# End of the second network: three down projections after the last gate/ups, and the lower parts of three tiles over TensorE

## Chip, cores and metric

One core of a Trainium2 chip. The metric is the device time of one execution in microseconds (us); the median of the runs before is 905.04 us.

## What is computed

x is 4096 rows (2 batches of 2048) of 256 numbers. Three stages follow each other, each on a layernorm of x and each added back to x: a feed-forward network, an attention, and the same feed-forward network again. Only the last stage's end is touched. The network is

```python
def fp4_linear(x, w):
    xq = fp4_quant_dequant(x)      # blocks of 16: scale max|x|/6, round to an 8 value grid
    wq = fp4_quant_dequant(w)
    return jnp.einsum('bsk,nk->bsn', xq, wq)
gate = fp4_linear(x, w_gate)       # 256 -> 704
y = fp4_linear(x, w_up)            # 256 -> 704
h = jax.nn.silu(gate) * y
return fp4_linear(h, w_down)       # 704 -> 256
```

and x becomes x + 0.5 * network(layernorm(x)).

## The kernel before

The rows lie in 32 tiles of 128 (NT = 32). A network (f = 0 or 1) is a software pipeline of rounds c, written by hand for each engine in its own queue; engines meet only at semaphores. In every round "chain" k is the quantised row of tile k's h (704 columns, for its down projection) and, where `ahead(k)` holds (k up to 27), of the normalised x of tile k + 4 (256 columns, for the gate/up of that tile, which is why the gate/up of tile c + 3 reads chain c - 1). Matrix products are made in two parts of reduced precision: an upper part `T_hi` and a lower part `T_lo` of the transposed data, against an upper and a lower part of the weights.

Round c of network 2, by engine:

- TensorE (PE): waits for the lower part of chain c - 1, and for `gu_read` (VectorE has read the gate/up result of tile c + 2, whose PSUM bank is written next); `gate_up` part 0 of tile c + 3 (6 matmuls of 512 columns, L1881); `transpose_chain(c)` (8 transposes, 6 where no x is ahead, L1762); part 1 (6 x 512); where `by_product` holds, `chain_lower(c)` (2 matmuls of 512 columns, L1920, that subtract `T_hi` in PSUM); part 2 (6 x 384); then the down projection of tile c into the single PSUM area `dn` (10 matmuls L1892 on `T_hi`, 7 matmuls L1899). It waits for `down_done`, that is for ScalarE's copy of the previous tile out of `dn`.
- ScalarE (ACT), in this order: `absolute(c+1)` (|y| of chain c + 1, L1407; of tile 31 L1398), `down_out(c-1)` (dn to SBUF, L1414), `chain_upper(c)` (L1425), `silu_gate(c+3)` (L1449), and where `by_product` holds `chain_rest(c)` (L1439, L1441: the lower part out of PSUM).
- VectorE (DVE): `scales(c+2)` (L811 to L824), `to_grid(c+1)` (L833 `rounded`, L839 `grid`), `scaled(c+2)` (L852), `lower(c)` where `by_vector` holds (L894, L896), `product(c+3)` (L798: silu times up, which sets `gu_read`).
- GpSimd (POOL): `residual(c-1)` (x plus down, L554), `quantised(c+1)` (`zq` = grid times scale, L587).
- SyncE: sends finished tiles of x to memory, the last four one by one.

`by_vector` holds in network 2 for chains 0 to 28; chain 29 goes over TensorE and ScalarE. Tiles 30 and 31 are "late": VectorE makes their zq (`quantised_late`, L918, L920) and lower parts (L904 to L910), TensorE's `last_two` does transposes of 30, upper down projection of 30 (L2012), transposes of 31, rest of 30 (L2021), and then both parts of 31 into a bank of its own. VectorE adds tile 31 to x (L927). `T_hi` and `T_lo` have two slots, used by the parity of k. `down_out(t)` also waits until the residual of tile t - 2 is done, because `down` has two slots.

Of the kernel before, what the change touches and what calls it, by code (L numbers as in the profile page):

```python
# [7 lines left out]
F32 = mybir.dt.float32  # L8
# [5 lines left out]
P = 128  # L14
# [16 lines left out]
def macaron_kernel(nc, x_in, wq, bq, wk, bk, wv, bv, wo, bo, w_gate, w_up, w_down, out):  # L31
# [35 lines left out]
    with ctx:  # L67
# [84 lines left out]
        plain.close()  # L152
        sb("slots_ahead_of_xk", [P, RING - 4, QT * P], at=plain)
# [148 lines left out]

        def by_vector(f, k):

            return isinstance(k, int) and (0 if f else 4) <= k < NT - 3
# [148 lines left out]
        def _(pool):  # L454
# [95 lines left out]
            def ffn_step(f):  # L550
# [162 lines left out]
        def _(dve):  # L713
# [77 lines left out]
            def ffn_step(f):  # L791
# [34 lines left out]
                def to_grid(k):  # L826

                    lo, hi = part(k)
                    y_k = z if last(k) else y
                    abs_k = silu[:] if last(k) else yabs_of(f, k, lo, hi)  # L830
# [8 lines left out]
                    nc.vector.scalar_tensor_tensor(out=grid[:, lo:hi], in0=abs_k, scalar=ROUND,  # L839
                                                   in1=rounded[:, lo:hi], op0=ALU.max,  # L840
                                                   op1=ALU.subtract).then_inc(grid_done, 1)
# [47 lines left out]
                def lower(k, par):  # L889
# [4 lines left out]
                    nc.vector.tensor_tensor(out=T_lo[:, par, n, :], in0=bank[:, n, :],  # L894
                                            in1=T_hi[:, par, n, :].bitcast(F32), op=ALU.subtract)
                    nc.vector.tensor_tensor(out=T_hi[HR:P, par, HK + KD, :], in0=bank[HR:P, HK + KD, :],  # L896
                                            in1=T_hi[HR:P, par, HK + KD, :].bitcast(F32),
                                            op=ALU.subtract).then_inc(vector_lo, 1)

                def lower_late(k, par):  # L900
# [3 lines left out]
                    nc.vector.tensor_tensor(out=T_lo[:, par, 0:4, :], in0=bank[:, 0:4, :],  # L904
                                            in1=T_hi[:, par, 0:4, :].bitcast(F32),
                                            op=ALU.subtract).then_inc(late_lo, 1)
                    dve.wait_ge(hi_done, number(f, k))
                    nc.vector.tensor_tensor(out=T_lo[:, par, 4:HK, :], in0=bank[:, 4:HK, :],
                                            in1=T_hi[:, par, 4:HK, :].bitcast(F32), op=ALU.subtract)
                    nc.vector.tensor_tensor(out=T_hi[HR:P, par, HK + KD, :], in0=bank[HR:P, HK + KD, :],  # L910
                                            in1=T_hi[HR:P, par, HK + KD, :].bitcast(F32),
                                            op=ALU.subtract).then_inc(late_lo, 1)

                def quantised_late(k, par):
# [3 lines left out]
                    nc.vector.tensor_tensor(out=blocks(zq[:, 0:I]), in0=blocks(grid[:, 0:I]),  # L918
                                            in1=spread(s_neg[:, par, 0:HB], HB), op=ALU.mult)
                    nc.vector.tensor_tensor(out=blocks(zq[:, I:I + HR]), in0=blocks(grid[:, I - HR:I]),  # L920
# [298 lines left out]
        def _(act):  # L1219
# [172 lines left out]
            def ffn_step(f):  # L1392
# [27 lines left out]
                def chain_upper(k, par):  # L1420
# [4 lines left out]
                    nc.scalar.activation(T_hi[:, par, t, :], bank[:, t, :], ACT.Copy).then_inc(hi_done, 1)  # L1425

                def late_upper(k, par):

                    bank = bank_of(k)
                    act.wait_ge(T_done, number(f, k))  # L1430
                    nc.scalar.activation(T_hi[:, par, 0:4, :], bank[:, 0:4, :], ACT.Copy).then_inc(late_hi, 1)
                    nc.scalar.activation(T_hi[:, par, 4:8:3, :], bank[:, 4:8:3, :], ACT.Copy).then_inc(hi_done, 1)

                def chain_rest(k, par):
# [4 lines left out]
                    last = nc.scalar.activation(T_lo[:, par, t, :], bank[:, t, :], ACT.Copy)  # L1439
                    if hidden(k):  # L1440
                        last = nc.scalar.activation(T_hi[HR:P, par, HK + KD, :], bank[HR:P, HK + KD, :], ACT.Copy)  # L1441
# [20 lines left out]
                def step(c, par):  # L1462
# [7 lines left out]
                    if c == NT - 2:  # L1470
                        down_out(c - 1, 1 - par)
                    if late(c) and chain(c):
                        late_upper(c, par)
                    if extra and c == NT - 1:
                        keys_upper(0, 0)
                    if hidden(c - 1) and c < NT and c != NT - 2:
                        down_out(c - 1, 1 - par)
                    if measured:
# [20 lines left out]
                    if extra and c == -2:  # L1499
                        query_row()  # L1500
                    if by_product(f, c):
                        chain_rest(c, par)
                    if extra and c == NT - 3:
# [252 lines left out]
        def _(pe):  # L1756
# [118 lines left out]
            def gate_up(par, part):  # L1875
# [3 lines left out]
                         for T, w in ((T_hi, w1_hi), (T_hi, w1_lo), (T_lo, w1_hi))]  # L1879
                for n, (T, kd, w) in enumerate(terms):  # L1880
                    last = nc.tensor.matmul(gu[:, lo:hi], lhsT=T[:, par, HK + kd, :], rhs=w[:, kd, lo:hi],  # L1881
# [6 lines left out]
            def project_down_first(par, dn):  # L1888

                terms = [(k, half) for k in range(HK) for half in (0, D)]  # L1890
                for n, (k, half) in enumerate(terms):
                    nc.tensor.matmul(dn, lhsT=T_hi[:, par, k, :], rhs=wd_hl[:, k, half:half + D],  # L1892
                                     start=n == 0, stop=False)

            def project_down_rest(par, dn):

                terms = [(T_hi, HK + KD, HK, half) for half in (0, D)] + [(T_lo, k, k, 0) for k in range(HK)]
                for n, (T, k, wk, half) in enumerate(terms):
                    last = nc.tensor.matmul(dn, lhsT=T[:, par, k, :], rhs=wd_hl[:, wk, half:half + D],  # L1899
# [15 lines left out]
            def chain_lower(f, c, par):  # L1915

                pe.wait_ge(hi_done, number(f, c))
                if hidden(c):
                    for bank in range(2):
                        last = nc.tensor.matmul(bank2[:, bank, :], lhsT=neg_ident[:],  # L1920
                                                rhs=T_hi[:, par, 4 * bank:4 * bank + 4, :],
                                                start=False, stop=True, skip_group_check=True)
                else:
                    last = nc.tensor.matmul(bank2[:, 1, P:3 * P], lhsT=neg_ident[:],
                                            rhs=T_hi[:, par, HK:HK + KD, :],
# [10 lines left out]
            def ffn_step(f):  # L1936
                def step(c, par):
# [7 lines left out]
                    if gated:  # L1945
                        pe.wait_ge(gu_read, NT * f + c + 3)
                        gate_up(1 - par, 0)
                    if gated and c < 0:
                        gate_up(1 - par, 1)
                        gate_up(1 - par, 2)  # L1950
# [15 lines left out]
                    if gated and c >= 0:  # L1966
                        gate_up(1 - par, 1)
# [9 lines left out]
                    if gated and c >= 0:  # L1977
                        gate_up(1 - par, 2)
                    if hidden(c):
                        if f and c == 0:  # L1980
                            pe.wait_ge(x_att, NT)
                        if f or c:
                            pe.wait_ge(down_done, (NT - 1) * f + c)
                        else:
                            pe.wait_ge(wc["lo"], len(groups))
                        pe.wait_ge(hi_done, number(f, c))
                        project_down_first(par, dn)
                        wait_lowered(f, c)
                        project_down_rest(par, dn)
# [13 lines left out]
                def down_late(par, dn):  # L2003
# [4 lines left out]
                    for k in range(HK):  # L2008
                        if k == 4:
                            pe.wait_ge(hi_done, number(f, NT - 2 + par))  # L2010
                        for half in (0, D):
                            nc.tensor.matmul(dn, lhsT=T_hi[:, par, k, :], rhs=wd_hl[:, k, half:half + D],  # L2012
                                             start=k == 0 and half == 0, stop=False)

                def down_late_rest(par, dn):

                    terms = [(T_lo, k, k, 0) for k in range(HK)] + [(T_hi, HK + KD, HK, half) for half in (0, D)]
                    for n, (T, k, wk, half) in enumerate(terms):
                        if n in (0, 4):
                            pe.wait_ge(late_lo, 4 * f + 2 * par + 1 + n // 4)  # L2020
                        last = nc.tensor.matmul(dn, lhsT=T[:, par, k, :], rhs=wd_hl[:, wk, half:half + D],  # L2021
# [50 lines left out]
            gate_up(0, 0)  # L2072
            key_query_lower()
            gate_up(0, 1)
            transpose_chain(0, -3)
            pe.wait_ge(aw["m_lo"], 1)
            gate_up(0, 2)
# [199 lines left out]
            gate_up(0, 0)  # L2277
            gate_up(0, 1)
# [7 lines left out]
            gate_up(0, 2)  # L2286
# [6 lines left out]
            for columns in range(3):  # L2293
                gate_up(1, columns)
# [6 lines left out]
            for columns in range(3):  # L2301
                gate_up(0, columns)
# [26 lines left out]
```

## Time and profile before

| | us |
|---|---|
| median of 3 runs (lowest, highest) | 905.04 (904.86, 905.08) |
| the profiled execution | 904.92 |
| its span, first to last instruction | 903.1 |
| PE / DVE / ACT / POOL busy in the span | 882.2 / 691.0 / 620.8 / 551.2 |

The span is what the trace covers; the execution's own time is 1.8 us more. Busy time is the union of an engine's instructions. Matmuls overlap in the records, so that the distance from one start to the next is their cost, not the duration shown. All times below are from the span's start.

### The profile page before, as it was taken

To read this page: it belongs to the slowest core of one execution; us is meant where nothing else is said; L and a number is where in the kernel's file an instruction comes from. 1 tells how busy PE (TensorE), PEld (TensorE's weight loads), DVE (VectorE), ACT (ScalarE), POOL (GpSimd) and SP (SyncE) were. 2 spreads that over 40 slices of the span, in tenths; PEclk is the share of its full clock that TensorE was granted. 3 is DMA by queue.
4 is the path that set the end of the run, shared out by engine and by line. 5 is a ranking of instruction groups with operands and counts; after the bars stand their busy time and mean duration, and the time that the engine had idled before them with its cause. 6 is when DMAs were issued, how large, how long until landed. Compare 5 with 4: busy or idle time off the path is not lost.

```text
span 903.1 us, 16183 instructions
## 1 busy us (share of the span) xinstructions
PE 882.2 (98%) x5608; PEld 795.6 (88%) x5608; DVE 691.0 (77%) x1086; ACT 620.8 (69%) x1383; POOL 551.2 (61%) x619
## 2 busy tenths in 40 slices
PE   4999999999999999999999999999999999999997
PEld 2789999999988899989998899998998999999996
DVE  7977999999977666555564644545599999999998
ACT  6789888887674765768675576767784667555453
POOL 5477889898420354536752154546577878877762
PEclk9999999999999999999999999999999999999999
DMA  9200000000000000000000000000000000000001
GB/s 314 68 1 1 1 1 2 1 1 1 1 1 0 1 1 1 1 1 2 1 1 1 1 1 1 1 1 1 1 1 1 1 24 24 25 24 24 1 24 47
DMA packets 11952, 13.81 MB, mean 15 GB/s; under 512 B 864, under 2 KB 11104, under 8 KB 11872
## 3 DMA queue, kind: packets, MB, share of 16 engines
q1 hardware_dynamic: 11872, 12.79, 4.3%
q8 instruction: 45, 0.74, 0.3%
q14 instruction: 35, 0.29, 0.1%
HBM read 8.59 MB, written 4.19 MB: 14 GB/s over the span
## 4 chain that ended last, share of the span: by engine, by line
PE 89%; DVE 4%; POOL 3%; issue 2%; ACT 1%; DMA 1%; SPq 0%; DVEq 0%; POOLq 0%
PE bank L1881 25%; PE bank L2137 19%; PE bank_b L1892 7%; PE bank L1762 7%; PE bank_b L1899 5%; PE bank L2175 5%; PE bank L2179 5%; PE bank L2177 5%; PE bank L2100 3%; POOL p_lo L637 2%; PE bank_b L2179 2%; PE bank_b L2175 2%; PE bank_b L2177 2%; PE bank L2118 1%; PE bank_b L2118 1%
## 5 line engine op out<-in xcount | busy, mean ns | idle before, releaser
L637 POOL TENSOR_TENSOR p_lo<-s_ring,p_hi 128x512 fp32r<-128x512 f32 x128 | 167.7, 1315 | 215.8 <-ACT p_hi L1620 215.7
L1004 DVE TENSOR_TENSOR top<-bank,top 128x512 f32<-128x512 f32 x98 | 67.7, 691 | 117.6 <-ACT s_ring L1604 117.6
L587 POOL TENSOR_TENSOR zq<-grid,s_neg 128x256 f32<-128x256 f32 (+2 forms) x184 | 142.0, 799 | 12.6 <-DVE grid L839 12.6
L1881 PE MATMUL bank<-w_hi,T_hi 128*128 128x512 f32 (+1 forms) x384 | 148.6, 387 | 0.4 <-DVE z L798 0.3
L1881 PE MATMUL bank<-w_hi,T_lo 128*128 128x512 f32 (+1 forms) x384 | 143.9, 375 | 0.0
L1881 PE MATMUL bank<-w_lo,T_hi 128*128 128x512 f32 (+1 forms) x384 | 143.5, 374 | 0.0
L1604 ACT ACTIVATE s_ring<-bank 128x512 f32<-128x512 f32 x128 | 76.0, 594 | 75.9 <-PE bank L2137 75.9
L1425 ACT ACTIVATE T_hi<-bank 128x1024 fp32r<-128x1024 f32 (+1 forms) x68 | 64.7, 952 | 84.6 <-PE bank L1762 84.6
L2175 PE MATMUL bank<-v_hl,p_hi 128*128 128x258 f32 x384 | 109.9, 286 | 0.4 <-DVE x L1037 0.2
L2179 PE MATMUL bank<-v_hl,p_lo 128*128 128x258 f32 x384 | 108.2, 282 | 0.0
L2177 PE MATMUL bank<-v_hl,p_hi 128*128 128x256 f32 x384 | 108.1, 282 | 0.0
L569 POOL TENSOR_TENSOR y<-z,s_inv 128x960 f32<-128x960 f32 (+1 forms) x56 | 99.6, 1779 | 5.3 <-DVE rounded L833 4.4
L2137 PE MATMUL bank<-q_hi,k_hi 128*128 128x512 f32 x256 | 100.8, 394 | 0.1
L2137 PE MATMUL bank<-q_lo,k_hi 128*128 128x512 f32 x256 | 100.5, 393 | 0.0
L2137 PE MATMUL bank<-q_hi,k_lo 128*128 128x512 f32 x256 | 100.2, 391 | 0.0
L1610 ACT ACTIVATE s_ring<-s_ring 128x512 f32<-128x512 f32 x128 | 79.2, 622 | 18.4 <-DVE s_ring L1027 18.4
L1027 DVE TENSOR_TENSOR s_ring<-s_ring,bank 128x512 f32<-128x512 f32 x128 | 84.8, 677 | 1.3 <-PE bank L1762 0.8
L1620 ACT ACTIVATE p_hi<-s_ring 128x512 fp32r<-128x512 f32 x128 | 80.7, 632 | 7.0 <-PE bank_b L2179 3.5
L811 DVE TENSOR_REDUCE amax<-z 128x60 f32<-128x960 f32 (+2 forms) x72 | 74.9, 1041 | 11.2 <-ACT z L1459 8.5
L1881 PEld LDWEIGHTS bank<-w_hi,T_lo 128*128 128x128 f32 x384 | 72.1, 188 | 10.6
L1881 PEld LDWEIGHTS bank<-w_hi,T_hi 128*128 128x128 f32 x384 | 72.2, 188 | 10.2 <-DVE z L798 0.9
L1892 PE MATMUL bank_b<-wd_hl,T_hi 128*128 128x256 f32 x600 | 80.4, 279 | 0.1
(241 smaller groups left out, 2237.1 us busy)
## 6 DMA issues: line engine op xcount, KB each, us to landing
out<-x SPq DMA_DIRECT2D x7, 512.0 KB, 2.9
x<-in_L_attn_hidden_states SPq DMA_DIRECT2D x3, 1024.0 KB, 12.2
x<-in_L_attn_hidden_states SPq DMA_DIRECT2D x2, 512.0 KB, 7.2
wraw<-in_L_ffn_w_down SPq DMA_DIRECT2D x1, 704.0 KB, 7.5
wraw<-in_L_ffn_w_up SPq DMA_DIRECT2D x1, 640.0 KB, 5.1
wq_s<-in_L_attn_Wq SPq DMA_DIRECT2D x1, 512.0 KB, 6.7
wk_s<-in_L_attn_Wk SPq DMA_DIRECT2D x1, 512.0 KB, 7.6
wo_s<-in_L_attn_Wo SPq DMA_DIRECT2D x1, 512.0 KB, 8.3
```

The costliest lines, as they stand in the source:

```text
L569: nc.gpsimd.tensor_tensor(out=blocks(y[:, lo:Z]), in0=blocks(z[:, lo:Z]), in1=spread(s_inv[:, lo // BLOCK:ZB], (Z - lo) // BLOCK), op=ALU. ...
L587: last = nc.gpsimd.tensor_tensor(out=blocks(zq[:, to:to + hi - lo]), in0=blocks(grid[:, lo:hi]), in1=spread(s_neg[:, par, lo // BLOCK:hi / ...
L637: nc.gpsimd.tensor_tensor(out=lower_buf(n, c), in0=score_buf(n, c), in1=upper_buf(n, c).bitcast(F32), op=ALU.subtract).then_inc(plo_done, 1)
L1027: nc.vector.tensor_tensor(out=p, in0=p, in1=shift_bank, op=ALU.subtract).then_inc(diff_done, 1)
L1610: nc.scalar.activation(p, p, ACT.Exp, scale=SCALE).then_inc(exp_done, 1)
L1620: nc.scalar.activation(upper_buf(n, c), score_buf(n, c), ACT.Copy).then_inc(phi_done, 1)
L1881: last = nc.tensor.matmul(gu[:, lo:hi], lhsT=T[:, par, HK + kd, :], rhs=w[:, kd, lo:hi], start=n == 0, stop=n == len(terms) - 1)
L1892: nc.tensor.matmul(dn, lhsT=T_hi[:, par, k, :], rhs=wd_hl[:, k, half:half + D], start=n == 0, stop=False)
L2137: last = nc.tensor.matmul(score_bank(c), lhsT=kk[:, kd, t], rhs=q[:, kd, :], start=i == 0, stop=i == len(terms) - 1)
L2175: nc.tensor.matmul(o[:, 0:D + 2], lhsT=hi[:, q], rhs=v_hl[:, c, 0:D + 2], start=c == 0, stop=False, skip_group_check=True)
L2177: nc.tensor.matmul(o[:, 0:D], lhsT=hi[:, q], rhs=v_hl[:, c, D + 2:], start=False, stop=False, skip_group_check=True)
L2179: last = nc.tensor.matmul(o[:, 0:D + 2], lhsT=lo[:, q], rhs=v_hl[:, c, 0:D + 2], start=False, stop=c == CH - 1, skip_group_check=True)
```

## The change

Network 2 only, at its end:

- `by_vector` now ends at chain 25: the lower parts of chains 26, 27 and 28 are made by `chain_lower` on TensorE and `chain_rest` on ScalarE, no longer by VectorE.
- `held` tiles 26, 27 and 28: their down projection, `down_out` and `residual` leave their own rounds. Round 29 of TensorE is now: down 26, transposes 29, down 27, `chain_lower(29)`; `last_two` is: down 28, transposes 30, down 29, transposes 31, upper down of 30, rest of 30, both parts of 31.
- Round 29 of ScalarE is now: `absolute(30)`, `down_out(26)`, `chain_upper(29)`, `down_out(27)`, `chain_rest(29)`, `down_out(28)`; round 30 starts with `absolute(31)` as before, then the upper parts of tile 30, then `down_out(29)`.
- Round 29 of GpSimd is now: `quantised(30)`, and then the residuals of 26, 27 and 28. VectorE no longer makes zq of tile 30.
- Tiles 28 to 31 have upper and lower buffers of their own (`last_hi`, `last_lo`).
- `to_grid(31)` writes into `y` and no longer waits for zq of the tile before (in both networks).

```diff
+        def in_last(f, k):
+            return f == 1 and isinstance(k, int) and k >= NT - 4
+        def held(f, k):
+            return f == 1 and isinstance(k, int) and NT - 6 <= k < NT - 3
         def by_vector(f, k):
-            return isinstance(k, int) and (0 if f else 4) <= k < NT - 3
+            return isinstance(k, int) and ((0 if f else 4) <= k < (NT - 6 if f else NT - 3))
...
                     # GpSimd, step(c, par)
-                    if hidden(c - 1) and c < NT:
+                    if hidden(c - 1) and c < NT and not held(f, c - 1):
                         residual(c - 1, 1 - par)
-                    if chain(c + 1) and not late(c + 1):
+                    if chain(c + 1) and not late(c + 1) or f and c == NT - 3:
                         quantised(c + 1, 1 - par)
+                    if f and c == NT - 3:
+                        residual(c - 3, 1 - par)
+                        residual(c - 2, par)
+                        residual(c - 1, 1 - par)
...
                     # VectorE, blocks_of(NT - 3) and to_grid
                         to_grid(NT - 2)
-                        quantised_late(NT - 2, 1 - par)
+                        if f == 0:
+                            quantised_late(NT - 2, 1 - par)
-                    if f or between(k, 1 - LEAD, NT - 1):
+                    if (f or between(k, 1 - LEAD, NT - 1)) and not last(k):
                         dve.wait_ge(zq_done, number(f, k) - 1)
...
                     # ScalarE, step(c, par)
+                    if f and c == NT - 3:
+                        down_out(c - 3, 1 - par)
                     if chain(c) and not late(c):
                         chain_upper(c, par)
...
+                    if f and c == NT - 3:
+                        down_out(c - 2, par)
                     if by_product(f, c):
                         chain_rest(c, par)
+                    if f and c == NT - 3:
+                        down_out(c - 1, 1 - par)
...
                     # TensorE, step(c, par) and last_two
+                    if f and c == NT - 3:
+                        project(c - 3)
                     transpose_chain(f, c)
+                    if f and c == NT - 3:
+                        project(c - 2)
...
                     pe.wait_ge(gu_read, NT * (f + 1))
+                    if f:
+                        project(NT - 4)
                     transpose_chain(f, NT - 2)
                     if f == 0:
                         transpose_keys(0, 0)
-                    down_late(0, dn)
+                    else:
+                        project(NT - 3)
+                    if f == 0:
+                        down_late(0, dn)
                     transpose_chain(f, NT - 1)
+                    if f:
+                        down_late(0, dn)
                     down_late_rest(0, dn)
```

## Rows read from the trace of the kernel before

**Rows 1.** The page, busy time of the engines.
```profile
PE 882.2 (98%) x5608; PEld 795.6 (88%) x5608; DVE 691.0 (77%) x1086; ACT 620.8 (69%) x1383; POOL 551.2 (61%) x619
```
**Rows 2.** Stretches: us, busy us by engine (count), PE clock, DMA share, GB/s.
```profile
875.19:881.87 6.68, 6.68 (x46) 6.12 (x44) 6.49 (x11) 2.83 (x4) 2.97 (x3) 1.00 0.00 0
...
888.34:900.50 12.16, 9.93 (x73) 8.55 (x71) 10.28 (x20) 5.90 (x11) 2.35 (x3) 1.00 0.07 24
...
902.00:903.10 1.10, 0.00 (x0) 0.00 (x0) 0.00 (x0) 0.00 (x0) 0.00 (x0) 0.79 0.23 75
```
**Rows 3.** PE in order of time: start, us, engine, line, operation [idle before].
```profile
876.57 1.03 PE L1762 MATMUL bank<-ident,zq 128*128 128x128 f32 x8
877.37 0.47 PE L1881 MATMUL bank<-w_hi,T_hi 128*128 128x512 f32 x1
...
878.83 0.33 PE L1881 MATMUL bank<-w_hi,T_hi 128*128 128x384 f32 x1
...
879.87 1.34 PE L1892 MATMUL bank_b<-wd_hl,T_hi 128*128 128x256 f32 x10
...
881.87 0.40 PE L1881 MATMUL bank<-w_hi,T_hi 128*128 128x512 f32 x1
...
883.25 0.82 PE L1762 MATMUL bank<-ident,zq 128*128 128x128 f32 x6
...
890.27 0.73 PE L1920 MATMUL bank<-T_hi,neg_ident 128*128 128x512 f32 x2 [1.11 <-ACT T_hi L1425]
890.83 1.34 PE L1892 MATMUL bank_b<-wd_hl,T_hi 128*128 128x256 f32 x10
...
896.63 0.87 PE L1762 MATMUL bank<-ident,zq 128*128 128x128 f32 x6
```
**Rows 4.** Stretch of one round of network 1, with chain_lower in it.
```profile
57.63:64.78 7.15, 7.15 (x46) 6.42 (x45) 4.95 (x7) 5.84 (x14) 5.19 (x7) 1.00 0.00 0
```
**Rows 5.** DVE in order of time, rounds 27 to the end.
```profile
880.21 0.89 DVE L798 TENSOR_TENSOR z<-bank,silu 128x704 f32<-128x704 f32 x1
...
886.60 0.89 DVE L798 TENSOR_TENSOR z<-bank,silu 128x704 f32<-128x704 f32 x1 [0.23 <-PE bank L1881]
...
889.15 1.32 DVE L852 TENSOR_TENSOR z<-z,s_inv 128x704 f32<-128x704 f32 x1
...
893.30 0.88 DVE L833 SCALAR_TENSOR_TENSOR rounded<-silu,z 128x704 f32<-128x704 f32 x1
894.21 1.30 DVE L839 SCALAR_TENSOR_TENSOR grid<-silu,rounded 128x704 f32<-128x704 f32 x1
895.55 0.89 DVE L918 TENSOR_TENSOR zq<-grid,s_neg 128x704 f32<-128x704 f32 x1
...
900.49 0.42 DVE L927 SCALAR_TENSOR_TENSOR x<-bank,x 128x256 f32<-128x256 f32 x1 [1.13 <-PE bank L2021]
```
**Rows 6.** ACT in order of time, rounds 27 to 29 and absolute(31).
```profile
877.65 1.03 ACT L1425 ACTIVATE T_hi<-bank 128x1024 fp32r<-128x1024 f32 x1 [1.87 <-PE bank L1762]
879.03 0.76 ACT L1449 ACTIVATE silu<-bank 128x704 f32<-128x704 f32 x1 [0.35 <-PE bank L1881]
879.68 0.75 ACT L1407 ACTIVATE bank<-y 128x704 f32<-128x704 f32 x1
...
891.03 0.92 ACT L1439 ACTIVATE T_lo<-bank 128x896 fp32r<-128x896 f32 x1 [0.82 <-PE bank L1920]
...
892.26 0.79 ACT L1398 ACTIVATE silu<-z 128x704 f32<-128x704 f32 x1
893.42 0.39 ACT L1414 ACTIVATE down<-bank_b 128x256 f32<-128x256 f32 x1 [0.37 <-PE bank_b L1899]
```
**Rows 7.** POOL's groups by form, 866 to 868.6 and 884 to 887.
```profile
L587 POOL TENSOR_TENSOR zq<-grid,s_neg 128x704 f32<-128x704 f32 x1 | 1.4, 1392 | 0.0
...
L587 POOL TENSOR_TENSOR zq<-grid,s_neg 128x704 f32<-128x704 f32 x1 | 2.0, 1978 | 1.2 <-DVE grid L839 1.2
```
**Rows 8.** POOL in order of time, the residual of tile 27.
```profile
889.00 0.72 POOL L554 TENSOR_TENSOR x<-x,down 128x256 f32<-128x256 f32 x1 [2.30 <-ACT down L1414]
```

More of the change, by code:

```diff
@@ L829, in to_grid @@
                     y_k = z if last(k) else y
+                    grid_k = y if last(k) else grid
                     abs_k = silu[:] if last(k) else yabs_of(f, k, lo, hi)
@@ L917, in quantised_late @@
                     dve.wait_ge(T_done, number(f, k - 1))
-                    nc.vector.tensor_tensor(out=blocks(zq[:, 0:I]), in0=blocks(grid[:, 0:I]),
+                    grid_k = y if last(k) else grid
+                    nc.vector.tensor_tensor(out=blocks(zq[:, 0:I]), in0=blocks(grid_k[:, 0:I]),
                                             in1=spread(s_neg[:, par, 0:HB], HB), op=ALU.mult)
-                    nc.vector.tensor_tensor(out=blocks(zq[:, I:I + HR]), in0=blocks(grid[:, I - HR:I]),
+                    nc.vector.tensor_tensor(out=blocks(zq[:, I:I + HR]), in0=blocks(grid_k[:, I - HR:I]),
                                             in1=spread(s_neg[:, par, HB - HR // BLOCK:HB], HR // BLOCK),
@@ L1424, in chain_upper @@
                     act.wait_ge(T_done, number(f, k))
[L1425 removed]
+                    nc.scalar.activation(hi_of(f, k)[:, t, :], bank[:, t, :], ACT.Copy).then_inc(hi_done, 1)
                 def late_upper(k, par):
@@ L1469, in step @@
                         normalise(6)
-                    if c == NT - 2:
+                    if c == NT - 2 and not f:
                         down_out(c - 1, 1 - par)
@@ L1873, in _, with gate_up @@
             pe.wait_ge(neg_set, 1)
-            def gate_up(par, part):
+            def gate_up(f, k, part):
                 lo, hi = ((0, 512), (512, 1024), (1024, G))[part]
                 terms = [(T, kd, w) for kd in range(KD)
-                         for T, w in ((T_hi, w1_hi), (T_hi, w1_lo), (T_lo, w1_hi))]
+                         for T, w in ((hi_of, w1_hi), (hi_of, w1_lo), (lo_of, w1_hi))]
                 for n, (T, kd, w) in enumerate(terms):
-                    last = nc.tensor.matmul(gu[:, lo:hi], lhsT=T[:, par, HK + kd, :], rhs=w[:, kd, lo:hi],
+                    last = nc.tensor.matmul(gu[:, lo:hi], lhsT=T(f, k)[:, HK + kd, :], rhs=w[:, kd, lo:hi],
                                             start=n == 0, stop=n == len(terms) - 1)
@@ L1886, in gate_up, with project_down_first, project_down_rest @@
                     last.then_inc(gu_done, 1)
[L1888 removed]
+            def project_down_first(f, c, dn):
                 terms = [(k, half) for k in range(HK) for half in (0, D)]
                 for n, (k, half) in enumerate(terms):
[L1892 removed]
+                    nc.tensor.matmul(dn, lhsT=hi_of(f, c)[:, k, :], rhs=wd_hl[:, k, half:half + D],
                                      start=n == 0, stop=False)
[L1895 to L1897 removed]
+            def project_down_rest(f, c, dn):
+                terms = [(hi_of, HK + KD, HK, half) for half in (0, D)] + [(lo_of, k, k, 0) for k in range(HK)]
                 for n, (T, k, wk, half) in enumerate(terms):
[L1899 removed]
+                    last = nc.tensor.matmul(dn, lhsT=T(f, c)[:, k, :], rhs=wd_hl[:, wk, half:half + D],
                                             start=False, stop=n == len(terms) - 1)
@@ L1966, in step @@
                     if gated and c >= 0:
-                        gate_up(1 - par, 1)
+                        gate_up(f, c - 1, 1)
                     if extra and c == NT - 3:
@@ L1977, in step, with project @@
                     if gated and c >= 0:
[L1978 to L1989, printed above, removed]
+                        gate_up(f, c - 1, 2)
+                    if f and c == 0:
+                        pe.wait_ge(x_att, NT)
+                    if hidden(c) and not held(f, c) and not (f and c == NT - 3):
+                        project(c)
+                def project(c):
+                    if f or c:
+                        pe.wait_ge(down_done, (NT - 1) * f + c)
+                    else:
+                        pe.wait_ge(wc["lo"], len(groups))
+                    pe.wait_ge(hi_done, number(f, c))
+                    project_down_first(f, c, dn)
+                    wait_lowered(f, c)
+                    project_down_rest(f, c, dn)
                 def last_two():
                     pe.wait_ge(gu_read, NT * (f + 1))
+                    if f:
+                        project(NT - 4)
                     transpose_chain(f, NT - 2)
@@ L2011, in down_late @@
                         for half in (0, D):
-                            nc.tensor.matmul(dn, lhsT=T_hi[:, par, k, :], rhs=wd_hl[:, k, half:half + D],
+                            nc.tensor.matmul(dn, lhsT=hi_of(f, NT - 2 + par)[:, k, :], rhs=wd_hl[:, k, half:half + D],
                                              start=k == 0 and half == 0, stop=False)
                 def down_late_rest(par, dn):
-                    terms = [(T_lo, k, k, 0) for k in range(HK)] + [(T_hi, HK + KD, HK, half) for half in (0, D)]
+                    terms = [(lo_of, k, k, 0) for k in range(HK)] + [(hi_of, HK + KD, HK, half) for half in (0, D)]
                     for n, (T, k, wk, half) in enumerate(terms):
@@ L2020, in down_late_rest @@
                             pe.wait_ge(late_lo, 4 * f + 2 * par + 1 + n // 4)
-                        last = nc.tensor.matmul(dn, lhsT=T[:, par, k, :], rhs=wd_hl[:, wk, half:half + D],
+                        last = nc.tensor.matmul(dn, lhsT=T(f, NT - 2 + par)[:, k, :], rhs=wd_hl[:, wk, half:half + D],
                                                 start=False, stop=n == len(terms) - 1)
@@ L2276, in _ @@
             wait_lowered(1, -4)
-            gate_up(0, 0)
-            gate_up(0, 1)
+            gate_up(1, -4, 0)
+            gate_up(1, -4, 1)
             weighted_values(n, 4)
@@ L2285, in _ @@
             pe.wait_ge(diff_done, CH * NQ)
-            gate_up(0, 2)
+            gate_up(1, -4, 2)
             weighted_values(n, 8)
@@ L2293, in _ @@
             for columns in range(3):
-                gate_up(1, columns)
+                gate_up(1, -3, columns)
             weighted_values(n, 10)
@@ L2301, in _ @@
             for columns in range(3):
-                gate_up(0, columns)
+                gate_up(1, -2, columns)
             for c in range(12, CH):
```

59 lines of the change are left out of this document (35 added, 24 removed).

## The prediction

> **What bounds the kernel now.** The page shows TensorE busy for 98% of the span [rows 1], so first of all the kernel is TensorE's queue. The stretches show where that ends: in a round of network 2 it is busy without a gap, 6.68 us of 6.68, with VectorE nearly as full at 6.49, while after the last gate/up it works only 9.93 of 12.16 us [rows 2]. There the chain that ends last runs through VectorE. Its product of tile 31 starts at 886.60, and zq of tile 31 (895.55) releases the last transposes at 896.63, after which TensorE is full until x at 900.49 [rows 3, 5]. The question is whether the change shortens that chain of VectorE, and whether TensorE has room for what is put there.
>
> **Costs from the rows.** From one start to the next on TensorE: gate/up part 0 1.38 (881.87 to 883.25), 8 transposes 0.80, part 1 1.46, part 2 1.04, one down projection 2.00 (879.87 to 881.87) [rows 3]. Six transposes are 6/8 of 0.80, 0.60. `chain_lower` inside a full round costs 0.47: the round of network 1 that has it takes 7.15 against 6.68 [rows 2, 4]. Restarted after a wait it took 0.56 (890.27 to 890.83) [rows 3]; I take 0.1 for every restart of TensorE behind a wait, with bounds of 0 and 0.15. Handovers: end of gate/up part 1 to silu 0.20 and end of transposes to upper part 0.28 [rows 3, 6]; I use 0.20 for `down_out` too. Part 2 of tile 31 ended at 883.25 + 0.60 + 1.46 + 1.04 = 886.35 and the product started at 886.60, so 0.25. From a product's start to the matmul that it releases: 0.89 [rows 5] and a handover that I estimate at 0.06, a little more than the 0.04 between VectorE's own dependent ops (894.21 + 1.30 to 895.55) [rows 5]; in all 0.95.
>
> **The gate/ups of tiles 30 and 31.** VectorE loses three lower parts, which only adds to its slack, and TensorE three down projections of 2.00. But the gate/up of the next tile overwrites the bank that the product reads, so it waits for `gu_read`. Before, the down projection lay in that gap and covered it; now nothing does. The last matmul of tile 29's gate/up ends at 875.19 - 2.00 + 0.47 = 873.66, its product starts at 873.91, and TensorE may begin tile 30 at 874.86 (before: 875.19). A round is then 0.10 + 1.38 + 0.80 + 1.46 + 0.47 + 1.04 = 5.25, plus 0.25 + 0.95 = 6.45, where it was 6.68. So tile 30's gate/up ends at 880.11 with the product at 880.36 (before 880.21), and tile 31's, with six transposes, starts at 881.31 and ends at 886.36, the product at 886.61 (before 886.60) [rows 3, 5]. **The last gate/up comes no earlier**: the first `chain_lower` costs 0.47 in a round whose down projection is not yet missed, and the two gaps of 1.2 us (0.25 + 0.95) give most of the rest away. ScalarE's `chain_rest` hides behind these gaps: chain 27's takes 1.23 (891.03 to 892.26) after a silu start plus 0.65 (879.03 to 879.68), done about 0.6 before tile 31's gate/up may start [rows 6].
>
> **TensorE after it.** Before, after 886.35, it had four down projections (28 to 31), 3 x 0.60 of transposes and 0.47: 10.27 us of work in 13.94, so 3.67 idle. Now it has six down projections, 14.27 us. Even without one wait it would end at 886.36 + 14.27 = 900.63, 0.34 later than before. With its waits: `gate_up` part 1 of tile 31 ends at 884.85, silu starts at 885.05, `chain_rest(28)` at 885.70 and ends at 886.93. TensorE waits for it at the head of round 29: down 26 from 886.99, with a restart to 889.09; transposes 29 to 889.69. `down_out(26)` (0.20 + 0.39 [rows 6] + 0.06) ends behind the transposes, so down 27 runs to 889.74 + 2.10 = 891.84. `chain_lower(29)` lies inside the next handover. Down 28 waits for `down_out(27)`: 891.84 + 0.65 = 892.49, to 894.59. All downs share one bank, so each one waits for ScalarE's copy of the last.
>
> **What is queued behind.** ScalarE's `down_out(28)` waits for down 28: 894.79 to 895.18. Behind it in ScalarE's own queue stands `absolute(31)`, whose input is ready near 890. Before, it ran at 892.26 [rows 6]. Now it runs from 895.18 to 895.97, and VectorE, which finished grid of tile 30 near 892, sits idle for it. Then `rounded` 0.91 and `grid` 0.91 of tile 31 (0.91 is the distance 893.30 to 894.21; the grid of before took 1.30, see below), from 896.0 to 897.82, and zq to the transposes 1.08 (895.55 to 896.63) [rows 3, 5]: transposes of 31 at 898.90, 2.27 later than 896.63. Down 29 has run between (895.24 to 897.34). Behind the transposes (0.65 with restart) now stand both whole late down projections, 4.00; the upper half of tile 30's used to be ahead of them. The last matmul ends at 903.55, x of tile 31 starts at 903.75 instead of 900.49: **3.26 later**.
>
> What is moved to GpSimd costs nothing here: zq of tile 30 takes 1.39 + 0.3 [rows 7] from near 892.0, done near 893.7, and the transposes of 30 come at 894.59. The three residuals behind it end near 895.9; `down_out(28)` needs that of 26, near 894.4, 0.4 ahead. If zq of 30 took 1.98, as one did [rows 7], this cover is gone and adds 0.2. SyncE's transfers follow the residuals: that of tiles 24 to 27 leaves near 895.3 and no longer near 889.7 [rows 8], eight us ahead of the end; tile 30's leaves about 1.2 ahead of tile 31's. So the end behind x stays as it was. Own buffers and the grid of 31 in `y` remove waits that nobody stands in; both cost 0.
>
> Sum: 904.92 for the profiled execution + 3.26 = **908.2 us**. The median shown is 0.12 above that execution; this is inside what I can resolve.
>
> **A lock between VectorE and GpSimd.** VectorE's z<-z took 1.32 when the residual of GpSimd had started 0.15 ahead of it, against 0.89 for the like zq<-grid [rows 5, 8]; grid<-silu took 1.30 where rounded<-silu of the same width took 0.88; GpSimd's zq took 1.98 in one round and 1.39 in another [rows 5, 7, 8]. So two ops of these engines with both inputs in SBUF follow one another, the later one waiting. In the forecast zq of tile 31 starts at 897.82 and the residual of tile 29 at about 897.99, so VectorE is first by 0.17. Were it the other way, it would wait up to 0.72 [rows 8]: 908.9. The Trainium skill, "SBUF — State Buffer", section "Who interferes with whom", states this as a rule: a VectorE op with two SBUF inputs and a GpSimd op that reads SBUF exclude each other, and whichever issues first keeps the shared port to its end. By that rule, this rival is decided by the order of two starts alone; the rows above agree with it.
>
> **Rivals.** (1) The lock falls the other way, 908.9; for it, 0.17 is less than my error. (2) `absolute(31)` does not decide. Then down 29 does: transposes 30 to 895.19, down 29 from 895.24 to 897.34, transposes to 897.94, 4.00, 0.20: x at 902.14, 1.65 later, 906.6. Against it: the order of the queue is written in the code, and VectorE has nothing else to do. (3) Nothing but TensorE's work counts, 905.3. Against it: the one `dn` bank. (4) Faster: the change does what it says, and gate/ups run ahead without gaps. They would end 2.62 earlier at 883.74, and without any wait behind them the end would be 883.74 + 14.27 + 0.20, 2.3 earlier: 902.6. It needs a round of gate/up and product under about 5.3 us; it decides where the product of a tile is read before that tile's part 2 has ended, which `gu_done` forbids. (5) The clock falls in one of TensorE's new gaps. Before it kept 1.00 through a gap whose engine part was 1.11 [rows 2, 3], and shows 0.79 only in the last stretch, after some 2 us without a matmul [rows 2]; the new gap ahead of the last transposes is 1.56. At the 1.2 GHz level the last 4.00 would take 8.00: about 912.
>
> **How the numbers follow.** Forecast 0.70, its own range 907.5 (no restart costs anything) to 908.9 (each costs 0.15, and GpSimd's 0.2); rival 1 0.14; rival 2 0.08; rival 3 0.03; rival 4 0.03; rival 5 0.02. A measurement of this kernel tells 0.2% (1.8 us) from no change; slower begins at 906.85. Slower 0.86, same (rivals 2 and 3) 0.11, faster 0.03. The range 906.6 to 909.2 takes in rivals 1 and 2 and leaves out the rest.
>
> **What would show it.** Product of 31 within 0.3 of 886.6; TensorE idle about 1.2 twice between the gate/ups; `absolute(31)` right behind `down_out(28)` near 895.2; VectorE idle some 3.5 us ahead of `rounded` of 31; z<-z of tile 31 at 0.88 to 0.9 and not 1.32; the last transposes near 898.9 and about 4.0 us of matmuls after them. I am wrong if the product of 31 starts before 885.5, if down projections don't wait for `down_out`, or if `absolute(31)` runs before 893.

## The result, and the profile after

The changed kernel takes 909.57 us (median of 6 executions, 909.0 to 910.9) against 905.06 before: slower, ratio 1.0051 (95% interval 1.0041 to 1.0061). The forecast was 908.2 with 906.6 to 909.2: right in direction and in its main waits, but 1.4 too low, and the measured time lies 0.4 above the range. The term that failed is the lock between VectorE and GpSimd, which was put at nothing and cost 0.53. The profiled execution took 909.34 with a span of 907.5, where that of before took 904.92 and 903.1.

VectorE after the change, in order of time, from the product of tile 28 to x of tile 31 (before: [rows 5]; line numbers are those of the changed kernel):

```profile
867.16 0.89 DVE L822 TENSOR_TENSOR z<-bank,silu 128x704 f32<-128x704 f32 x1
...
880.90 0.89 DVE L822 TENSOR_TENSOR z<-bank,silu 128x704 f32<-128x704 f32 x1 [1.58 <-PE bank L1916]
...
887.25 0.89 DVE L822 TENSOR_TENSOR z<-bank,silu 128x704 f32<-128x704 f32 x1 [1.37 <-PE bank L1916]
...
889.79 0.89 DVE L877 TENSOR_TENSOR z<-z,s_inv 128x704 f32<-128x704 f32 x1
890.72 0.89 DVE L858 SCALAR_TENSOR_TENSOR rounded<-bank,y 128x704 f32<-128x704 f32 x1
891.64 0.89 DVE L864 SCALAR_TENSOR_TENSOR grid<-bank,rounded 128x704 f32<-128x704 f32 x1
896.54 0.89 DVE L858 SCALAR_TENSOR_TENSOR rounded<-silu,z 128x704 f32<-128x704 f32 x1 [4.00 <-ACT silu L1425]
897.46 0.89 DVE L864 SCALAR_TENSOR_TENSOR y<-silu,rounded 128x704 f32<-128x704 f32 x1
898.39 0.89 DVE L945 TENSOR_TENSOR zq<-y,s_neg 128x704 f32<-128x704 f32 x1
899.20 0.75 DVE L947 TENSOR_TENSOR zq<-y,s_neg 128x64 f32<-128x64 f32 x1
...
904.89 0.42 DVE L954 SCALAR_TENSOR_TENSOR x<-bank,x 128x256 f32<-128x256 f32 x1 [2.15 <-PE bank L2071]
```

GpSimd in order of time, the residual of tile 29 (the lock below rests on it):

```profile
898.57 1.29 POOL L574 TENSOR_TENSOR x<-x,down 128x256 f32<-128x256 f32 x1 [2.00 <-ACT down L1441]
```

VectorE sits idle for 4.00 us ahead of `rounded` of tile 31, released by ScalarE's `absolute(31)`. ScalarE in order of time shows why (before: [rows 6]):

```profile
895.37 0.39 ACT L1441 ACTIVATE down<-bank_b 128x256 f32<-128x256 f32 x1 [1.09 <-PE bank_b L1934]
895.65 0.79 ACT L1425 ACTIVATE silu<-z 128x704 f32<-128x704 f32 x1
```

`absolute(31)` runs right behind `down_out(28)`, although its input, VectorE's z<-z, was ready at 890.7. TensorE in order of time, the gap between two gate/ups, and the tail (before: [rows 3]):

```profile
873.86 0.34 PE L1916 MATMUL bank<-w_hi,T_lo 128*128 128x384 f32 x1
875.37 0.47 PE L1916 MATMUL bank<-w_hi,T_hi 128*128 128x512 f32 x1 [1.17 <-DVE z L822]
...
895.80 1.45 PE L1927 MATMUL bank_b<-wd_hl,last_hi 128*128 128x256 f32 x10
...
900.00 0.87 PE L1797 MATMUL bank<-ident,zq 128*128 128x128 f32 x6 [1.93 <-DVE zq L947]
900.63 1.42 PE L2062 MATMUL bank_b<-wd_hl,last_hi 128*128 128x256 f32 x10
```

And the stretches of that engine (columns as in [rows 2]): one gate/up round, the tail.

```profile
875.37:881.93 6.56, 5.39 (x28) 4.38 (x29) 4.88 (x9) 3.52 (x5) 2.22 (x2) 1.00 0.00 0
886.94:904.89 17.95, 15.48 (x123) 14.39 (x122) 10.74 (x19) 7.66 (x16) 6.24 (x9) 1.00 0.13 45
```

TensorE's round lost the 2.0 us down projection and gained a `chain_lower` of 0.47, yet it became only 0.12 shorter than the 6.68 of [rows 2]: of its 6.56 only 5.39 are busy, and 1.17 are the wait for the product. The product in turn waited for TensorE (1.58 and 1.37 idle on VectorE), so gate/up and product follow one another here.

Executions begin the changed part at different times: the product of tile 28 starts at 866.78 before and at 867.16 after. So the stretch from that product to x of tile 31 is what is compared below. The stretch is 33.71 before (866.78 to 900.49) and 904.89 - 867.16 = 37.73 after: **4.02 longer**. It splits at two points that both traces have. Up to the product of 31: 19.82 before, 20.09 after, +0.27. From there to the last transposes: 10.03 and 12.75, +2.72. From them to x: 3.86 and 4.89, +1.03.

### The profile page after: what moved, and what is told of

It reads as the page before. It is cut to its first block, busy times and chain, and to the rows that moved or that the text cites. A ratio compares the mean times of both kernels' runs of the same rounds, so it can differ in the third digit from the quotient of the medians.

```text
span 907.5 us, 16188 instructions
## 1 busy us (share of the span) xinstructions
PE 884.0 (97%) x5614; PEld 796.1 (88%) x5614; DVE 687.8 (76%) x1078; ACT 624.0 (69%) x1389; POOL 552.3 (61%) x621
## 4 chain that ended last, share of the span: by engine, by line
PE 89%; DVE 5%; issue 2%; POOL 2%; ACT 2%; DMA 1%; SPq 0%; DVEq 0%; POOLq 0%; ACTq 0%
PE bank L1916 24%; PE bank L2187 19%; PE bank_b L1927 8%; PE bank L1797 7%; PE bank_b L1934 5%; PE bank L2229 4%; PE bank L2225 4%; PE bank L2227 4%; PE bank L2150 2%; PE bank_b L2229 1%; PE bank_b L2225 1%; PE bank_b L2227 1%; PE bank L2168 1%; PE bank_b L2168 1%; POOL p_lo L661 1%
## 5 line engine op out<-in xcount | busy, mean ns | idle before, releaser
L1452 ACT ACTIVATE T_hi<-bank 128x1024 fp32r<-128x1024 f32 (+1 forms) x66 | 62.6, 949 | 83.5 <-PE bank L1797 83.5
L1916 PEld LDWEIGHTS bank<-w_lo,T_hi 128*128 128x128 f32 x384 | 72.3, 188 | 8.6
```

What stands on the lines that cost most here:

```text
L1916: last = nc.tensor.matmul(gu[:, lo:hi], lhsT=T(f, k)[:, HK + kd, :], rhs=w[:, kd, lo:hi], start=n == 0, stop=n == len(terms) - 1)
```

## Experiments

Each was timed beside the kernel before on one chip, and the ratio is to that kernel; "stretch" is the one just defined, from the experiment's profile.

**1. `absolute(31)` early.**

```diff
                     if f and c == NT - 3:
+                        absolute(NT - 1)
                         down_out(c - 2, par)
...
-                    if chain(c + 1) and (f or not last(c + 1)) and (f or c != -1):
+                    if chain(c + 1) and not last(c + 1) and (f or c != -1):
...
                     # VectorE, to_grid
+                    if f and last(k):
+                        dve.wait_ge(grid_done, number(f, k) - 1)
```

> The changed kernel with absolute(31) on ScalarE in round 29 ahead of down_out(27), and with VectorE waiting for its own grid of tile 30 before rounded of tile 31. Queue theory (absolute(31) stuck behind down_out(28) sets the end): absolute(31) near 891.9, rounded(31) near 892.6, and the last transposes then wait for down 29 on TensorE: near 898.0 instead of 900.0; x of tile 31 about 2.0 earlier (902.9), time about 907.5. Rival (TensorE merely has too much work after the last gate/up, the queue position is no cause): x stays within 0.3 of 904.9, time 909.3.

908.49 us, ratio to before 1.0036 (1.0023 to 1.0049); stretch 904.23 - 867.51 = 36.72, 1.01 less than the changed kernel. Half of what was expected. The rival (no cause) falls, but the 2.0 did not come. VectorE of this run, in order of time:

```profile
892.99 2.13 DVE L860 SCALAR_TENSOR_TENSOR rounded<-silu,z 128x704 f32<-128x704 f32 x1
895.16 0.89 DVE L866 SCALAR_TENSOR_TENSOR y<-silu,rounded 128x704 f32<-128x704 f32 x1
```

GpSimd of the same run, in order of time:

```profile
892.98 2.29 POOL L607 TENSOR_TENSOR zq<-grid,s_neg 128x704 f32<-128x704 f32 x2 [5.25 <-DVE grid L866]
895.24 3.45 POOL L574 TENSOR_TENSOR x<-x,down 128x256 f32<-128x256 f32 x3
```

And ScalarE of the same run:

```profile
896.73 0.38 ACT L1443 ACTIVATE down<-bank_b 128x256 f32<-128x256 f32 x1 [2.09 <-POOL x L574]
```

Now `rounded` of 31 meets GpSimd's zq of tile 30 (2.13 for 0.89), and `down_out(28)` waits for GpSimd's residual of tile 26, which stands behind that zq and itself takes 1.40, beside VectorE's `grid` of 31. That stops down 29 on TensorE for 0.82. Part of the wait had only moved.

**2. Upper down projection of tile 30 ahead of the last transposes.**

```diff
+                    if f:
+                        down_late(0, dn)
                     transpose_chain(f, NT - 1)
-                    if f:
-                        down_late(0, dn)
```

> The changed kernel with the upper down projection of tile 30 put back ahead of the transposes of tile 31. Placement theory: it fits into TensorE's idle 1.93 us ahead of those transposes (it can start at 898.55, when down_out(29) is done, and ends at 899.8), so x of tile 31 is 1.2 earlier (903.7), time about 908.3. Rival (the work is only moved, the end is bound by something else): no change, 909.3 to 909.6.

908.46 us (1.0021 to 1.0049); stretch 903.69 - 866.98 = 36.71, 1.02 less. It fits into the idle time, as expected but for 0.2: its end (899.84) came just behind zq, and the rest of tile 30 then waited a little for its lower part. This is the +1.03 of the last piece of the split.

**3. The residual of tile 29 behind zq of tile 31.**

```diff
                     pool.wait_ge(down_done, (NT - 1) * f + t + 1)
+                    if f and t == NT - 3:
+                        pool.wait_ge(zq_done, number(1, NT - 1))
```

> The changed kernel with one wait more on GpSimd: the residual of tile 29 waits for zq of tile 31. Lock theory: the 64 column piece of zq took 0.75 because the residual (898.57, 1.29 us) ran; without it 0.22, the last transposes 0.53 earlier, x 904.4, time about 0.5 less, 908.9. Rival (the slow piece has another cause, such as the input in y): the piece stays at 0.75 and the time at 909.4.

908.96 us (1.0028 to 1.0053); stretch 904.16 - 867.03 = 37.13, 0.60 less. The 64 column piece of zq falls from 0.75 to 0.22 although its input is still `y`, so it was GpSimd's residual that held it:

```profile
898.19 0.89 DVE L947 TENSOR_TENSOR zq<-y,s_neg 128x704 f32<-128x704 f32 x1
899.00 0.22 DVE L949 TENSOR_TENSOR zq<-y,s_neg 128x64 f32<-128x64 f32 x1
```

**4. The kernel before with only the lower parts of 26 to 28 over TensorE.**

```diff
-            return isinstance(k, int) and (0 if f else 4) <= k < NT - 3
+            return isinstance(k, int) and (0 if f else 4) <= k < (NT - 6 if f else NT - 3)
```

> The kernel before with only the lower parts of chains 26 to 28 moved to TensorE and ScalarE; down projections stay in their rounds. Cost theory: three chain_lower of 0.47 each lengthen TensorE's full rounds, product of 31 at 888.0, everything behind it later by 1.4: time 906.4. Rival (VectorE, at 6.49 us of 6.68, is the real bound of the rounds, and taking 1.4 us off it in each pays for the matmuls): product of 31 at 886.6 or before, time 905.0 or less.

906.62 us (1.0007 to 1.0025); stretch 902.24 - 867.10 = 35.14, 1.43 more than before for three times 0.47. VectorE then idled 1.66, 2.17 and 1.95 ahead of its products: its relief bought nothing. The product of 31 starts 21.27 behind that of 28, 1.45 later than before.

**5. The changed kernel with those lower parts back on VectorE.**

```diff
-            return isinstance(k, int) and ((0 if f else 4) <= k < (NT - 6 if f else NT - 3))
+            return isinstance(k, int) and ((0 if f else 4) <= k < NT - 3)
```

> The changed kernel with the lower parts of chains 26 to 28 back on VectorE; the down projections stay held back. Measured from product of 28 to x of 31 (before 33.71 us, changed 37.73). Round theory (gate/up, product and VectorE's round each take about 6.45, so neither part of the change alone brings the gate/ups forward): product of 31 about 19.8 behind product of 28, as before, TensorE starts down 26 right at the end of the last gate/up, about 0.5 earlier than in the changed kernel; 37.2 in all, time 909.0. Rival (the three chain_lower, 1.41 us, are what it costs): 36.3, time 908.1.

908.86 us (1.0032 to 1.0057), 0.7 less than the changed kernel. The product of 31 starts 19.60 behind that of 28 (before 19.82, changed 20.09), so holding the down projections back brings the last gate/up forward by 0.2 here. The reason is another one than in the changed kernel: with the lower parts, VectorE runs without a gap from the product of 29 to that of 31, 6.44 a round, and TensorE waits for it (1.45 and 1.52). With the lower parts on TensorE, holding the down projections back takes 1.2 off experiment 4's 21.27, which pays for most of the three `chain_lower` and for no more. The profiled execution (910.31) shows something else besides. TensorE of this run, in order of time, behind the idle 1.93 us:

```profile
899.41 1.26 PE L1797 MATMUL bank<-ident,zq 128*128 128x128 f32 x6 [1.93 <-DVE zq L947]
900.33 2.48 PE L2062 MATMUL bank_b<-wd_hl,last_hi 128*128 128x256 f32 x10
```

The same engine's stretches in that run (columns as in [rows 2]; the granted clock is the number ahead of the last two):

```profile
898.00:899.40 1.40, 0.00 (x0) 0.00 (x0) 1.40 (x3) 0.00 (x0) 1.28 (x1) 1.00 0.17 56
899.40:900.30 0.90, 0.89 (x6) 0.89 (x7) 0.89 (x3) 0.00 (x0) 0.00 (x0) 0.70 0.14 50
900.30:901.00 0.70, 0.70 (x5) 0.70 (x4) 0.16 (x1) 0.29 (x1) 0.00 (x0) 0.50 0.37 123
901.00:902.00 1.00, 1.00 (x7) 1.00 (x7) 0.66 (x2) 0.58 (x2) 0.00 (x0) 0.50 0.00 0
902.00:903.00 1.00, 1.00 (x6) 1.00 (x6) 0.52 (x3) 0.00 (x0) 0.00 (x0) 0.50 0.00 0
903.00:904.00 1.00, 1.00 (x10) 1.00 (x9) 0.00 (x0) 0.10 (x1) 0.00 (x0) 0.92 0.00 0
```

The granted clock is at its lower level (1.2 GHz) from about 899.7 to 903.1, and the ten matmuls of the upper down projection take 2.48 instead of 1.42. From the last transposes to x it is 905.90 - 899.41 = 6.49 against 4.89: 1.60 lost. Without that the stretch would be 38.55 - 1.60 = 36.95, 0.78 less than the changed kernel, where 0.5 was expected; the rival (1.41 less) does not fit.

**6. The kernel before with the residuals out of VectorE's way.**

```diff
                     pool.wait_ge(down_done, (NT - 1) * f + t + 1)
+                    if f and t == NT - 4:
+                        pool.wait_ge(y_done, scaled_apart(1, NT - 1))
+                    if f and t == NT - 3:
+                        pool.wait_ge(zq_done, number(1, NT - 1))
```

> The kernel before with two waits more on GpSimd: the residual of tile 28 waits for VectorE's scaled of tile 31 (y_done), that of tile 29 for zq of tile 31. Lock theory: z<-z goes from 1.32 to 0.89 and grid<-silu from 1.30 to 0.89, both on the chain that ends last; 0.84 less on VectorE, 0.1 of it given back at the upper down projection of tile 30; 33.71 becomes 33.0, time 904.3. Rival (the two ops are slow for another reason, such as z written in place): both stay at 1.3 and the time at 905.3.

904.58 us (11 executions, 904.41 to 904.98) against 905.12, ratio 0.9994 (0.9985 to 1.0003); stretch 900.14 - 866.96 = 33.18, 0.53 less than before. Both ops fall to 0.89 (before [rows 5]: 1.32 and 1.30):

```profile
889.34 0.89 DVE L856 TENSOR_TENSOR z<-z,s_inv 128x704 f32<-128x704 f32 x1
...
893.34 0.89 DVE L837 SCALAR_TENSOR_TENSOR rounded<-silu,z 128x704 f32<-128x704 f32 x1 [0.20 <-ACT silu L1402]
894.26 0.89 DVE L843 SCALAR_TENSOR_TENSOR grid<-silu,rounded 128x704 f32<-128x704 f32 x1
```

Of the 0.84 gained on the two ops, 0.54 arrive at zq of 31; 0.20 VectorE gives back waiting for `absolute(31)`. The time agrees in size, but its interval still holds 1.

**7. `absolute(31)` early and zq of tile 30 back on VectorE.** The edits of experiment 1, and

```diff
-                        if f == 0:
-                            quantised_late(NT - 2, 1 - par)
+                        quantised_late(NT - 2, 1 - par)
...
-                    if chain(c + 1) and not late(c + 1) or f and c == NT - 3:
+                    if chain(c + 1) and not late(c + 1):
```

> The changed kernel with absolute(31) early (as in the first experiment) and zq of tile 30 back on VectorE, so that GpSimd's residuals of 26 to 28 stand behind nothing. Theory: now only TensorE's own queue is left, transposes of 31 right behind down 29; from product of 28 to x of 31 35.7 (37.73 - 2.0), time 907.5. Rival (the residual of tile 26 was not what held down_out(28)): 36.7 as in the first experiment, 908.5.

907.45 us (1.0015 to 1.0034); stretch 902.79 - 867.06 = 35.73, as expected. TensorE is now without a wait ahead of the last transposes, which follow down 29 at once:

```profile
895.72 1.44 PE L1929 MATMUL bank_b<-wd_hl,last_hi 128*128 128x256 f32 x10
897.00 0.39 PE L1936 MATMUL bank_b<-wd_hl,last_hi 128*128 128x256 f32 x2
897.23 0.75 PE L1936 MATMUL bank_b<-wd_hl,last_lo 128*128 128x256 f32 x5
897.82 0.82 PE L1799 MATMUL bank<-ident,zq 128*128 128x128 f32 x6
```

So with the stalls behind the last gate/up taken out, the order of the change is still 2.02 longer than before: that is TensorE's own queue, work and the waits between the gate/ups (1.17 and 1.18) that the change uncovered.

**8. The changed kernel again.** No edit.

> The changed kernel again, on the chip of these runs. Product of 28 to x of 31 37.7 again; what lies ahead of it within 0.4 of the kernel before; time 909.3 to 909.6. If the first runs were odd ahead of the change, it comes out near 909.1 (905.04 + 4.02).

909.52 us against 905.12; stretch 905.53 - 867.79 = 37.74, equal to 0.01. The start of the stretch varied by 0.6 between the two profiles of one kernel.

**9. TensorE's idle stretch filled.**

```diff
                     if f:
+                        for _ in range(7):
+                            nc.tensor.matmul(bank5[:, 2, :], lhsT=neg_ident[:], rhs=w1_hi[:, 0, 0:512],
+                                             start=True, stop=True, skip_group_check=True)
                     transpose_chain(f, NT - 1)
```

> The changed kernel with seven matmuls of 512 columns, whose result nobody reads, in TensorE's idle 1.93 us ahead of the transposes of 31 (7 x 0.23 = 1.6 us). Clock theory (in some executions the granted clock falls to its lower level behind that idle stretch, as in the profile of the fifth experiment, and costs some 1.5 us): product of 28 to x of 31 stays 37.7, but no execution lies more than 0.8 above the fastest, where the changed kernel had 3 of 11 that did (909.0 to 910.98); median 909.2. Rival (the slow executions come from elsewhere): the scatter stays.

909.51 us, all five between 909.24 and 909.78; stretch 904.85 - 867.18 = 37.67. The wait ahead of the transposes is 0.30 instead of 1.93. None of the five is a high one, but five are few: of the changed kernel's 11 executions 4 lie more than 0.8 above the fastest (909.97, 910.2, 910.9, 910.98; the expectation counts 3), so none of five has a chance of (7/11)^5 = 0.10 anyway. The median did not fall to 909.2.

The mean granted clock of each execution says more. 3.4 us at half the clock, as in experiment 5's profile, lower the mean of 908 us to 0.998. That is the mean of 910.9 and 910.98, and of experiment 5's two highest (910.31, 910.01); 909.97 and 910.2 have 1.000, so those two are not the clock. Of the 16 executions of the two kernels with the idle 1.93, 4 have 0.998; of the 30 of experiments 1, 2, 3, 7 and 9, with at most 1.42 idle ahead of the last transposes, none has. So the clock explains the highest executions, as far as a mean can tell, and not the rest of the scatter. Experiment 9 alone does not settle it.

**10. Experiment 6 with `absolute(31)` ahead of `chain_rest(29)`.**

```diff
-                    if chain(c + 1) and (f or not last(c + 1)) and (f or c != -1):
+                    if chain(c + 1) and not last(c + 1) and (f or c != -1):
                         absolute(c + 1)
...
+                    if f and c == NT - 3:
+                        absolute(NT - 1)
                     if by_product(f, c):
                         chain_rest(c, par)
```

> The kernel before with the residuals late (as in the sixth experiment) and absolute(31) ahead of chain_rest(29) on ScalarE. Theory: VectorE no longer waits 0.20 for absolute(31), but TensorE's upper down projection of tile 30 (to 896.2) then stands ahead of the last transposes just as long; gain 0 to 0.1 over the sixth experiment, time 904.5. Rival (VectorE still sets the last transposes): 0.2 gained, 904.4, and the transposes 0.2 earlier.

904.57 us (11 executions, 904.28 to 904.88) against 904.99, ratio 0.9994 (0.9985 to 1.0003); stretch 899.96 - 866.90 = 33.06. VectorE's zq of 31 comes 0.30 earlier in the stretch than in experiment 6, x only 0.12: TensorE's upper down projection of tile 30, which the last transposes now follow at once, has taken over.

## Why the forecast was right, and where it failed

From the product of tile 28, in us:

| | forecast | measured |
|---|---|---|
| product of 30 | 13.58 | 13.74 |
| product of 31 | 19.83 | 20.09 |
| `absolute(31)` | 28.40 | 28.49 |
| `rounded` of 31 | 29.22 | 29.38 |
| last transposes | 32.12 | 32.84 |
| x of 31 | 36.97 | 37.73 |

- **The last gate/up comes no earlier: right.** A round is gate/up, then product, then the next gate/up into the same bank, and taking the down projection out only uncovers the product: the trace has that wait twice, 1.17 each. Experiments 4 and 5 show that neither half of the change brings it forward by more than 0.2, the second because VectorE's own round of 6.44 is then the limit. A second gate/up bank was not tried.
- **`absolute(31)` queued behind `down_out(28)`: right.** It runs at 28.49 against 28.40. From `grid` of tile 30 to `rounded` of 31 it takes 4.90 (891.64 to 896.54), where it took 1.87 before with zq of tile 30 in between.
- **The upper half of tile 30 behind the last transposes: right**, 1.03 by the split, 1.02 by experiment 2. This and the stalls overlap; they don't add up with experiment 7's 2.02.
- **The step that failed is the lock**, in the forecast's terms the 1.08 from zq to the transposes, which measured 1.61 (898.39 to 900.00). I treated the lock as one decision (rival 1): zq of tile 31 starts 0.17 ahead of the residual of tile 29, so it costs nothing, or it waits up to 0.72. Both starts were forecast well (the residual started 0.18 behind zq), but zq is two instructions. GpSimd waited for the first (its residual took 1.29) and then held the second, of 64 columns, for 0.53 more: 0.75 for 0.22. Experiment 3 gives 0.60 back. This is the largest part of the 0.76 by which the stretch was under-estimated. The trace before has the same sequence. There the residual of tile 29 starts while VectorE's `rounded` of 31 (893.30, 0.88 [rows 5]) runs, and it is the next op, `grid`, that takes 1.30. GpSimd of the kernel before, in order of time:

```profile
893.88 0.88 POOL L554 TENSOR_TENSOR x<-x,down 128x256 f32<-128x256 f32 x1 [4.16 <-ACT down L1414]
```

  The Trainium skill, "SBUF — State Buffer", section "Who interferes with whom", says of the shared pair of ports that whoever issues first gets it "for the whole instruction". The trace agrees both ways round: GpSimd's residual waited out one VectorE instruction (1.29 for 0.73), and VectorE's next one waited out the residual (0.75 for 0.22).
- **Handovers mis-sized**: the other 0.23, of which 0.16 have come by `rounded` of 31. A product releases the next gate/up after 1.03 (874.34 to 875.37) where I used 0.95; TensorE's transposes, `chain_lower` and gate/ups ran as forecast.
- **Rival 2 was priced wrongly too.** I gave 1.65 later than before (906.6) if `absolute(31)` did not decide. Experiment 1 shows that moving it alone leaves 3.01, because zq of tile 30 on GpSimd then meets `rounded` and holds up `down_out(28)` through the residual of tile 26. I had written that zq on GpSimd costs nothing and that the residual of 26 was 0.4 ahead; that was cover given by the very stall. Without both it is 2.02 (experiment 7), TensorE's queue alone.
- **Rival 5, the clock**: in the fifth experiment's profile the granted clock fell behind an idle 1.93 and cost 1.60. Two of the changed kernel's own executions, 910.9 and 910.98, have the same mean clock of 0.998, but no profile of them was kept. Its chance of 0.02 was too small, and I forecast a gap of 1.56 where it is 1.93; the median is not an execution of this kind.
- **Outside the stretch**, where the forecast had nothing, lie 909.57 - 905.06 - 4.02 = 0.49. With the 0.76 and the 0.14 by which the median before (905.06) lies above the profiled execution, that is the 1.39 by which 904.92 + 3.26 was too low. Neither the lock nor this part alone would have taken the time out of the range. In the profile 0.38 of it are ahead of the product of tile 28. Some 0.14 to 0.22 of that arise near 510 us, in the attention: VectorE's small `shift` starts 0.43 behind `mr` (509.89 and 510.32) where it was 0.20 before (509.75 and 509.95), and TensorE's transposes of `shift` wait for it. That step is in all eight profiles of the changed kernel and of kernels made from it, and in none of the four of the kernel before and of kernels made from it. The rest was not traced; the start varied by 0.6 between two profiles of the changed kernel. Why an edit at the end moves something at 510 us stays open.
- A slip in the rows and in the forecast: the residual at 889.00 [rows 8] is that of tile 28, not 27. The transfer of tiles 24 to 27 left near 883.3 before and at 895.7 after; as forecast it costs nothing, x of 31 to the span's end is 2.61 in both.

So the gain that was sought went nowhere: the 2.0 us down projections had been the cover of a 1.2 us wait that this order of gate/up and product has with one bank. What was moved came back as 2.02 in TensorE's queue and 2.0 of stalls behind the other engines. What may gain goes the other way, experiments 6 and 10: about 0.5 us less than before, seen in the traces op by op, but each interval still holds 1.

## What to carry to other kernels

Before moving work out of a loop, ask which wait it covers there; if the next round needs a buffer that another engine has still to read, the time stays and the work comes on top at the end. When an instruction that waits late is put into an in-order queue, list what is already behind it, and again after each stall that you remove in thought, since a stall also covers the next one. The lock between VectorE and GpSimd counted per instruction here: an op that is split in two can win the first half and lose the second.

## What had not been expected of the hardware

An idle stretch of TensorE of 1.93 us was followed by the lower clock level in one profile and not in two others of the same shape (1.00 throughout in the changed kernel's two), at a price of 1.60 us; by their mean clock, 4 of 16 such executions had it. And a VectorE op with both inputs in SBUF lost 1.24 us (2.13 for 0.89) to one GpSimd op that was given out 0.01 ahead of it (892.98 and 892.99, experiment 1).
